# Pair products and decay matrices at the end of the first half, or at the head of the second

## The reference

```python
x = L0_attn_x                                       # (16, 256, 128)
h = layernorm(x) * (1 + ca) + sa
x = x + ga * mamba(h)          # a_: convolution, selective scan over 16 states, gate
h = layernorm(x) * (1 + cb) + sb
x = x + gb * moe(h)            # b_: shared and 8 routed experts, top 2
# second layer
h = layernorm(x) * (1 + ca) + sa
x = x + ga * delta_rule(h)     # c_: gated delta rule, 8 heads, key 128, value 32
h = layernorm(x) * (1 + cb) + sb
x = x + gb * attn_moe(h)       # d_: attention, then 8 dense experts of 512

# the gated delta rule, step by step over the tokens, per head:
S = S * exp(g_t)
u = (v_t - k_t S) * b_t
S = S + k_t u^T
o_t = q_t S
```

## Time and profile before

| what | value |
|---|---|
| median of three runs | 3085.35 us |
| the profiled execution | 3073.01 us, its span 3071.2 us |
| PE busy | 2502.6 us (81%) |
| DVE busy | 2245.6 us (73%) |
| ACT, POOL busy | 1247.8 us (41%), 641.2 us (21%) |
| mean granted clock of TensorE | 0.906 |

### The profile page before, as it was taken

How to read it: one execution, slowest core, us unless ns; L and a number is a source line. 1 busy time by engine, 2 the same in 40 slices (tenths; PEclk the granted TensorE clock), 3 DMA queues, 4 the chain that set the end, 5 groups by cost and what they waited for, 6 DMA issues and landing times.

```text
span 3071.2 us, 61542 instructions
## 1 busy us (share of the span) xinstructions
PE 2502.6 (81%) x22808; PEld 2004.1 (65%) x22808; DVE 2245.6 (73%) x5056; ACT 1247.8 (41%) x2761; POOL 641.2 (21%) x528
## 2 busy tenths in 40 slices
PE   2477978879887887978889797887988788897897
PEld 1166766757766576766757676575766657676686
DVE  1668777787877778787687877778787777877762
ACT  0233533435344253533425353243534424353342
POOL 0222122131212222122131212313121122202210
PEclk9869989989899898989989998998989989898998
DMA  4000000000000000000000000000000000000000
GB/s 119 2 2 3 2 8 3 7 3 7 2 3 8 2 7 3 6 2 3 7 3 7 2 3 8 3 7 3 7 2 3 7 3 7 3 4 5 1 5 2
DMA packets 24718, 21.52 MB, mean 7 GB/s; under 512 B 7210, under 2 KB 21443, under 8 KB 24403
## 3 DMA queue, kind: packets, MB, share of 16 engines
q1 hardware_dynamic: 24402, 17.14, 2.0%
HBM read 15.00 MB, written 2.13 MB: 6 GB/s over the span
## 4 chain that ended last, share of the span: by engine, by line
PE 60%; DVE 18%; issue 13%; POOL 4%; ACT 3%; SPq 1%; DMA 1%; DVEq 0%; POOLq 0%; ACTq 0%
PE banks L984 8%; PE banks L1160 8%; PE banks L1150 8%; PE banks L1034 6%; PE banks L918 4%; PE banks L927 3%; DVE wide L1332 3%; PE banks L976 3%; DVE wide L1344 2%; PE banks L855 2%; PE banks L962 2%; PE banks L1019 2%; PE banks L1026 2%; PE banks L897 2%; POOL lg L536 2%
## 5 line engine op out<-in xcount | busy, mean ns | idle before, releaser
L532 POOL TENSOR_TENSOR wide<-wide 128x512 f32<-128x512 f32 x128 | 243.5, 1902 | 872.5 <-DVE wide L1352 560.7
L1461 DVE SCALAR_TENSOR_TENSOR wide<-pad,conv,wide 128x256 f32<-128x256 f32 x864 | 389.1, 518 | 0.0
L984 PE MATMUL banks<-inv,mats 64*64 64x64 f32 x5120 | 198.0, 237 | 141.8 <-DVE inv L1505 104.6
L1344 DVE TENSOR_TENSOR_SCAN wide<-wide 128x1024 f32<-128x1024 f32 x128 | 308.4, 2409 | 1.9 <-ACT wide L634 0.3
L634 ACT ACTIVATE wide<-small,a_neg 128x255 f32<-128x255 f32 x512 | 217.8, 497 | 201.8 <-DVE wide L1344 198.9
L984 PEld LDWEIGHTS banks<-inv,mats 64*64 64x64 f32 x5120 | 185.2, 152 | 160.1 <-issue 159.2
L1150 PE MATMUL banks<-inv,up 128*128 128x256 f32 x1024 | 264.9, 387 | 0.0
L1160 PE MATMUL banks<-down,inv 128*128 128x128 f32 x2048 | 257.7, 277 | 0.0
L768 ACT ACTIVATE inv<-banks,up1b 128x256 f32<-128x256 f32 x512 | 215.0, 481 | 105.0 <-PE banks L1150 104.8
L1160 PEld LDWEIGHTS banks<-down,inv 128*128 128x128 f32 x2048 | 249.9, 192 | 5.8
L984 PE MATMUL banks<-inv 64*64 64x64 f32 x5120 | 189.0, 233 | 29.0 <-DVE inv L1513 28.9
(11 more groups left out here) (281 smaller groups left out, 5160.1 us busy)
## 6 DMA issues: line engine op xcount, KB each, us to landing
gates_bc<-gate_rows SPq DMA_DIRECT2D x32, 128.0 KB, 2.9
up<-in_W SPq DMA_DIRECT2D x1, 2048.0 KB
x<-in_x SPq DMA_DIRECT2D x16, 128.0 KB, 2.1
out<-xn_y SPq DMA_DIRECT2D x16, 128.0 KB, 1.9
wide<-in_wmod SPq DMA_DIRECT2D x2, 384.0 KB
con<-in_con SPq DMA_DIRECT2D x1, 724.0 KB
w_k<-in_Wk SPq DMA_DIRECT2D x1, 512.0 KB
w_q<-in_Wq SPq DMA_DIRECT2D x1, 512.0 KB
```

The costliest lines, as they stand in the source:

```text
L532: g.tensor_tensor(ypart[p % 2], r[:, 0:512], r[:, 512:1024], ALU.add).then_inc(a_yp.h, 1)
L984: last = t.matmul(PS[a:b, out, h * HALF:(h + 1) * HALF], weights(h, a, b), values(h, a, b), start=True, stop=True)
L1344: v.tensor_tensor_scan(state[st % 2], decay[st % 2], drive[st % 2], 0.0, ALU.mult, ALU.add).then_inc(a_h.h, 1)
L1461: v.scalar_tensor_tensor(dst, src, w, dst, ALU.mult, ALU.add).then_inc(c_conv.h, 1)
```

## The change

The pairs (c_gmask, c_logd, c_prod, c_unit) leave PROJECT and become PAIRS, the head of the second half. In the loop they are now done one pass later, for sequence i-1. They move out of the first half's buffers and banks: gmask and et lie in `inv`, c_logd writes bank 5 and c_prod banks 3 and 4. Three waits are added (a_turn, a_in, c_soft2; the waits of the first products go), so that the first half of i does not overwrite what the pairs of i-1 still read. c_unit's one-column operation is replaced by a count on a semaphore. All four strings of TURNS are new, so every step's place relative to the other half may differ.

```diff
-PROJECT = [("c_norm",), ("c_norm2",), ("c_turn",), ("c_ba",), ("c_beta",), ("c_soft",), ("c_soft2",), ("c_gmask", 0), ("c_gmask", 1)]
+PROJECT = [("c_norm",), ("c_norm2",), ("c_turn",), ("c_ba",), ("c_beta",), ("c_soft",), ("c_soft2",)]
...
+PROJECT += [("c_roots",)]
+PAIRS = [("c_gmask", 0), ("c_gmask", 1)]
 for gr in range(GROUPS):
-    PROJECT += [("c_logd", gr), ("c_prod", gr, 0), ("c_prod", gr, 1), ("c_unit", gr)]
+    PAIRS += [("c_logd", gr), ("c_prod", gr, 0), ("c_prod", gr, 1), ("c_unit", gr)]
     if gr + 2 < GROUPS:
-        PROJECT += [("c_gmask", gr + 2)]
-PROJECT += [("c_roots",)]
+        PAIRS += [("c_gmask", gr + 2)]
...
-SECOND_HALF = INVERT + APPLY + ATTEND + EXPERTS
+SECOND_HALF = PAIRS + INVERT + APPLY + ATTEND + EXPERTS
...
     "gpsimd": (
-        "xxxxxxxxxxyxyxxyxxxxxxxxxxxx"),
+        "yyxyyyxyyyxxxxxxxxxyxyxyxxx"),
...
-        gmask = [wide[:, 3, 512 * n:512 * n + 512].rearrange("p (h t) -> p h t", t=P) for n in range(2)]
-        et = [wide[:, 4, 512 * n:512 * n + 512].rearrange("p (h t) -> p h t", t=P) for n in range(2)]
...
+        gmask = [inv[:, n].rearrange("p (h t) -> p h t", t=P) for n in (10, 11)]
+        et = [inv[:, n].rearrange("p (h t) -> p h t", t=P) for n in (2, 9)]
...
                 g.wait_ge(c_MT.h, c_MT.at(i, 4 * gr + 4))
-                g.tensor_tensor(unit_gate[:, gr:gr + 1], zero_col, zero_col, ALU.add)
+                g.sem_inc(unit_free, 1)
...
             def turn_x(i, n, bk):
...
+                if n == 0 and not isinstance(i, int):
+                    t.wait_ge(c_vtok.h, c_vtok.at(i - 1, 1))
...
             def a_in(i):
                 t.wait_ge(ln_h[0].h, ln_h[0].at(i, 1))
+                if not isinstance(i, int):
+                    t.wait_ge(c_eGS.h, c_eGS.at(i - 1, 1))
...
                 t.wait_ge(c_gm.h, c_gm.at(i, gr + 1))
-                if gr == 0:
-                    t.wait_ge(c_ss.h, c_ss.at(i, 1))
-                else:
+                if gr >= 1:
                     t.wait_ge(c_et.h, c_et.at(i, gr))
-                t.matmul(bank(2), con[:, C_GT:C_GT + P], gmask[gr % 2].rearrange("p h t -> p (h t)"), start=True, stop=False)
+                t.matmul(bank(5), con[:, C_GT:C_GT + P], gmask[gr % 2].rearrange("p h t -> p (h t)"), start=True, stop=False)
...
-                if n == 0:
-                    t.wait_ge(c_vtok.h, c_vtok.at(i, 1))
-                elif n == 1:
-                    t.wait_ge(c_eGS.h, c_eGS.at(i, 1))
-                else:
+                if n >= 2:
                     t.wait_ge(c_AT.h, c_AT.at(i, n - 1))
...
-                    last = t.matmul(bank(n % 2, 256, y * 256), kq[:, h, 0, ch * P:(ch + 1) * P],
+                    last = t.matmul(bank(3 + n % 2, 256, y * 256), kq[:, h, 0, ch * P:(ch + 1) * P],
...
                 softplus16(i, 1, lg2)
+                if not isinstance(i, int):
+                    v.wait_ge(c_gm.h, c_gm.at(i - 1, GROUPS))
```

More of the change, by code:

```diff
@@ L123 @@
 FIRST_HALF = SCAN + ROUTED + PROJECT
-SECOND_HALF = INVERT + APPLY + ATTEND + EXPERTS
+SECOND_HALF = PAIRS + INVERT + APPLY + ATTEND + EXPERTS
 TURNS = {
     "tensor": (
-        "yyyyyyyyyxyxyyyyyyxyyxyyyyyyyyyyyxyyyyxxyyyxxyxxyxxyxxyxxyyxxxxxxxxyyxxyyxxyxxxxyxxyyyyxyxxyxyyx"
-        "yxyyyyyyyyyyyxyyxyyxyyxyyxyyxyyxyyyyyxxxxxxxxxxxxxxxxx"),
+        "yyyyyyyyyyyyxyxyyyyyyyyyyyxxyyyyyyyyyyxyyxxxyyxyyyyyxxyyyxyyxyxxyyxxyxxxxxyxxyxxxyyxxxxxyxxyyxyy"
+        "yxyyxxyyxyxyyyyyxyyyyxyyxyyxyyxyxyyyxyyyxxxyyyyyyyxyxx"),
     "vector": (
-        "yyyyyyxyxyyyxyyxyxyyxyxyyyyxyyyyxxxyyxyxxyxxxyxxxyxyxxyxyxxxxxyxxxyyxxyxxyxxyxxyxxxxyxyyxyxxxyxy"
-        "xyxxyxxyxxyxyxyyxxxxxxxxx"),
+        "xxyyyyyyyyyxyyyyyyxyyyxyyxyxyyyxyxyxxyyxxyyyxxyxyyyxxyxyxxxxyxxxxyxxyxxyxxyxxxxyxyxxyxxyyyxxxyyx"
+        "yyxxxyxxyxxxxyxxyxxyxyyyy"),
     "scalar": (
-        "yyyyyxyyxyyyyxxyyyyxyxyyyxyyyxyxyyxxxyxxxyxxyyxxyxxxxyyxyyyxxxyxyyyyxyyxyxyxyxyxyxyxyyxxxxxxxxxx"),
+        "yyyyxyyyxyyxxyyyyyyxyxxxyyxyyyyyyyxyyyyxxxyxxxxyxxxxyxyyxyyxxyyxyxyyxyxyyxyxyxxyxyxyyxxyyxyxyxxx"),
     "gpsimd": (
-        "xxxxxxxxxyxyxxyxxxxxxxxxxxx"),
+        "yyxyyyxyyyxxxxxxxxxyxyxyxxx"),
 }
@@ L334, in build @@
         released = sem("inversion_step_released")
+        unit_free = sem("diagonal_step_released")
         x_loaded = sig("x_loaded", 16)
@@ L700, in c_logd @@
                     s.wait_ge(c_AT.h, c_AT.at(i, 2 * (gr - 1)))
-                s.activation(et[gr % 2].rearrange("p h t -> p (h t)"), bank(2), ACT.Exp).then_inc(c_et.h, 1)
+                s.activation(et[gr % 2].rearrange("p h t -> p (h t)"), bank(5), ACT.Exp).then_inc(c_et.h, 1)
             def keep_x(i):
@@ L957, in c_logd @@
                 t.wait_ge(c_gm.h, c_gm.at(i, gr + 1))
-                if gr == 0:
-                    t.wait_ge(c_ss.h, c_ss.at(i, 1))
-                else:
+                if gr >= 1:
                     t.wait_ge(c_et.h, c_et.at(i, gr))
-                t.matmul(bank(2), con[:, C_GT:C_GT + P], gmask[gr % 2].rearrange("p h t -> p (h t)"), start=True, stop=False)
-                t.matmul(bank(2), identb[:], hideb[:].unsqueeze(1).broadcast_to([P, HG, P]), start=False, stop=True).then_inc(c_D.h, 1)
+                t.matmul(bank(5), con[:, C_GT:C_GT + P], gmask[gr % 2].rearrange("p h t -> p (h t)"), start=True, stop=False)
+                t.matmul(bank(5), identb[:], hideb[:].unsqueeze(1).broadcast_to([P, HG, P]), start=False, stop=True).then_inc(c_D.h, 1)
             def c_prod(i, gr, half):
@@ L1487, in c_prod @@
                     hh = 2 * half + y
[L1489 removed]
+                    v.scalar_tensor_tensor(MT[gr][:, hh, :], bank(3 + n % 2, P, y * 256), negc[:, ch, hg * HG + hh:hg * HG + hh + 1],
                                            et[gr % 2][:, hh, :], ALU.mult, ALU.mult).then_inc(c_MT.h, 1)
                 v.tensor_tensor(AT[gr][:, 2 * half:2 * half + 2, :],
[L1492 removed]
+                                bank(3 + n % 2).rearrange("p (y k t) -> p y k t", y=2, k=2)[:, :, 1, :],
                                 et[gr % 2][:, 2 * half:2 * half + 2, :], ALU.mult).then_inc(c_AT.h, 1)
```

3 lines of the change are left out of this document (removed).

## The result

The kernel after takes 3172.4 us (3165.0 to 3177.4, 4 runs) against 3085.4 us (4 runs) of before: 1.0281 times as long, 95% interval 1.0259 to 1.0302. Slower; forecast was 3062 us. The profiled execution took 3170.75 us, its span is 3169.0 us, and TensorE's mean granted clock fell from 0.906 to 0.874.

The account below looks back on a forecast made before the run. No engine is full over a pass; PE bounds stage A, DVE with its waits stage C. Stages 55.3 + 20.9 + 106.2 = 182.4 against 183.9 us, -23 us in 15 passes: 3085.4 to 3062 us, range 3035 to 3079.

Parts of the forecast that it names:

- Stage A: End of b_out to end of c_decay, projections beside experts, PE full: 55.3 us a pass forecast, 54.2 before.
- Stage C: Levels, scan, routed experts, attention up to the next b_out: 106.2 us forecast, 112.4 before; DVE work 81.2, listed waits 23.1.
- levels and the scan's head: DVE waits in the inversion's levels and the scan's start: 6.9 us a pass walked, 10.8 before.
- scan and apply: DVE waits in scan and apply: 4.9 us a pass walked, 2.5 before.
- routing: DVE waits in routing, behind b_norm2 and for the root: 5.4 us a pass walked, 5.0 before.
- hidden layer and attention: DVE waits in the routed experts' hidden layer and attention, up to b_out: 5.9 us a pass walked, 6.3 before.
- Stage B: End of c_decay to the inversion's first transpose: 20.9 us forecast, 17.3 before; first product 4.6 us after c_decay, products 10.3.
- any pitch but 2.9 us: Sign in stage B: product steps at a pitch other than 2.9 us a group would make the forecast wrong outright.
- The ends: First half alone sheds its pairs, second half alone takes them on: nothing in sum, within 2 us.
- The first: Rival at the loop's jump: PE's restart comes into the open, up to 4.4 us a pass, 3102 to 3128 us; chance 0.14.
- The second: Rival in routing and attention: serial chains stand bare on DVE, C 4.1 us longer, 3093 to 3124 us; chance 0.20.
- The third: Rival: the levels' waits go almost wholly under the scan, C gains another 3 us, 3018 us; chance 0.12.

Follow-up runs that it names:

- coef_fill: The kernel after plus 16 unused filling matmuls ahead of b_coef and one ahead of each b_up from the second: 3103.6 us, 1.0068 of before.
- turn_fill: The kernel after plus only 14 unused filling matmuls ahead of b_turn: 3154.6 us, 1.0233 of before.
- jump_fill: The kernel after plus 12 unused filling matmuls directly behind c_decay, ahead of the loop's jump: 3158.4 us, 1.0234 of before.

## Why the prediction was wrong

**Stage A** was right: 55.0 us where 55.3 were forecast (54.2 before).

**Stage C is the step that failed.** Its DVE work was right (81.4, forecast 81.2), its waits were not: DVE is idle 110.7 - 81.4 = 29.3 us, where 23.1 + 1.9 = 25.0 were forecast. Sorted by the walk's own terms, the listed waits are 27.4 us where it had 23.1: levels and the scan's head 8.0 (walked 6.9), scan and apply 2.7 (4.9), routing 5.8 (5.4), hidden layer and attention 10.9 (5.9). This last term is the one that was mis-sized, by 5.0 us; the errors of the other three (+1.1, -2.2, +0.4) nearly cancel, which is luck. Between b_coef and b_out, where this term lies, DVE is idle 19.6 - 8.4 = 11.2 us, and 14.7 - 8.4 = 6.3 us with the clock held (coef_fill). The difference, 4.9 us, covers the 4.3 us by which DVE's idle time was missed, and with the clock held the waits listed in the stretch come to 5.7 us, near the walked 5.9. The walk went through the new order with durations from the rows of before. But the new order changes the durations: it takes d_turn and d_qkv from between b_logits and b_coef, PE stands idle 4.0 us there, and b_up then runs at 1.2 GHz. The clock ahead of b_coef was already down in after, since the idle time ahead of b_turn; but turn_fill, which holds it up to b_logits, sees it at 1.2 GHz again when b_coef starts, and keeps the 19.2 us. The forecast had the clock of C in its rows (0.85) and did not ask what held it in the place that matters.

**Stage B** was 2.2 us too short (23.1, forecast 20.9). The first product starts 5.7 us after c_decay, not 4.6: DVE's jump took 2.58 us, not the 1.98 of the earlier trace rows, and began 0.4 us later, behind d_res. The products take 11.1 us, not 10.3, since the first group runs at the low clock behind the jump: its pitch on DVE is 3.7 us (1534.12 to 1537.84), where the forecast had called any pitch but 2.9 us wrong outright (jump_fill gives 1.0 us back). The remaining 0.3 us lie in c_first and a_conv. The restart of DVE and PE was foreseen, the fall of the clock in it was not.

**The base was a long pass.** The stages of before summed to 183.9 us, its passes have a mean of 182.5. Its passes alternate. Windows from the end of a_dt to the end of a_out in two neighbouring ones, the second of them within the C that was cut:
```profile
1340.78:1400.00 59.22, 45.92 (x532) 37.05 (x532) 54.48 (x60) 23.56 (x48) 19.49 (x10) 0.91 0.01 1
1523.27:1584.90 61.63, 48.83 (x518) 39.11 (x514) 55.03 (x60) 23.57 (x48) 18.98 (x10) 0.86 0.00 1
```
The long one has 15.0 us of PE's work at 1.2 GHz, the short one 8.5. The new stages were summed at 182.4: against the mean pass the forecast was no gain at all, and the -23 us came wholly from the pass that I had cut. That is 1.35 x 15 = 20 us of the error.

Together: -0.3 + 2.2 + 4.5 = 6.4 us a pass over the forecast's 182.4, 188.8 in sum, 188.7 measured. **The ends** cost 6 us where nothing was forecast; how they split was not tried. Stages 94, base 20 and ends 6 make the 120 us by which the profiled execution missed; the medians missed by 110, since the profiled execution of before lay further under its median than that of after.

**The rivals.** The first (PE's restart in the open) had the mechanism, but PE's jump is 2.7 us, under the 3.8 us from which it decides, and DVE waits 0.23 us for the first product, under the 0.5 us that was its sign. The second named the right place, routing and attention, and the right size (4.1 us on C), with the wrong mechanism: d_v waits 1.0 us, not 3.85, b_out costs 0.8 us, not 4.0, and with the clock held C is 106.2 us (110.7 - 4.5), the very forecast. The third did not hold: the levels' own waits fell to 4.9 us, but with the wait for the x-projection (L1300, 1.9) and those of the scan's drive (L1333, 1.2) the term came to 8.0 us, not to the 3.9 that it needed. The Trainium skill, "Runtime: NRT & Kernel Launch", section "Instruction fetch mechanics", was cited for the stall at a taken branch: the 2.69 us on PE and the 2.58 us on DVE agree, while ACT's row shows no stall; the prediction counted it as agreeing, and it is no support. That matmuls queued ahead of it cover the stall is shown by jump_fill.

Of 87 us lost against before, then, about 66 are the clock in the routed experts (the ratios of after and coef_fill, 1.0281 - 1.0068, times 3083), well outside the intervals. The clock behind the jump is worth some 15: 1.0 us a pass in jump_fill's ledger, and 14 us by its ratio (1.0234), though that interval touches after's. The rest was not taken apart. coef_fill is still 0.7% slower than before, so the clock alone does not account for the gain that was forecast and did not come: for that stand the base, stage B and the ends.

## What to carry to other kernels

Before a walk through a new order with old durations, look where the matrix engine will stand idle for some microseconds and what is due right behind: its work there can take twice as long, and this costs time where others wait for it. A few unused matmuls in such gaps (0.22 us each) were worth about 2%, 1% and 0.5% in three places of after; in before they gained 0.5% in one place and lost 0.5% in another. Take the base of a sum from the mean pass, not from the one that was cut: in before two neighbouring passes differ by some 2.5 us.
